# q, k and v of the neighbourhood attention projected from the transposed raw residual in fp32, with centred weights

## The reference, cut to what matters

```python
def _ln_c(v, eps=1e-06):
    m = jnp.mean(v, axis=1, keepdims=True)
    s = jnp.var(v, axis=1, keepdims=True)
    return (v - m) / jnp.sqrt(s + eps)
...
qkv = jnp.einsum('bchw,oc->bohw', x, qkv_w) + qkv_b[None, :, None, None]
qkv = qkv.reshape(B, 3, ND, d, H, W)
...
    qr = q.reshape(B, h, HEAD_DIM, L)
    ku = _unfold(kmap, dil).reshape(B, h, HEAD_DIM, KK, L)
    vu = _unfold(vmap, dil).reshape(B, h, HEAD_DIM, KK, L)
    attn = jnp.einsum('bhcl,bhcpl->bhlp', qr, ku) * SCALE
...
x = x + _L1_conv_ref(_ln_c(x), L1_conv_qkv_w, L1_conv_qkv_b, ...)
```

## Time and profile before

| | |
|---|---|
| median of 3 runs | 477.91 us (475.59 to 477.93) |
| profiled execution, its own time | 474.62 us |
| its span | 472.8 us |
| DVE busy | 403.7 us, 85% |
| PE busy | 359.8 us, 76% |
| ACT, POOL busy | 208.9 us, 136.2 us |
| mean granted clock of PE | 0.865 |

### The profile page before, as it was taken

The page is one execution under the profiler, slowest core; times in us unless marked ns, Lnnn a source line. Parts: engine busy times, 40 slices in busy tenths (PEclk is TensorE's granted clock), DMA queues, the critical chain, the costliest instruction groups (busy, mean ns, idle before and its releaser), DMA issues.

```text
span 472.8 us, 8901 instructions
## 1 busy us (share of the span) xinstructions
PE 359.8 (76%) x3276; PEld 196.9 (42%) x3276; DVE 403.7 (85%) x1349; ACT 208.9 (44%) x398; POOL 136.2 (29%) x133
## 2 busy tenths in 40 slices
PE   2856688968879656799999996680479869169996
PEld 1533543425328522356666663270134322024553
DVE  4787887898979788879999999888886888888997
ACT  1650125522310121388887883520036344128994
POOL 3630002002000000088888874021000006703442
PEclk9977879989977768899999997985589976579999
DMA  8800000000000000000000000000000000100000
GB/s 339 348 1 0 1 0 3 0 2 0 0 0 1 1 0 1 1 2 3 1 3 1 2 3 1 1 1 0 1 1 0 2 0 20 27 0 2 12 14 24
DMA packets 2859, 9.72 MB, mean 21 GB/s; under 512 B 512, under 2 KB 1152, under 8 KB 2688
## 3 DMA queue, kind: packets, MB, share of 16 engines
q1 hardware_dynamic: 1296, 5.21, 2.8%
q10 hardware_dynamic: 1008, 3.42, 1.8%
q0 software_dynamic: 512, 0.53, 0.5%
HBM read 8.63 MB, written 0.52 MB: 19 GB/s over the span
## 4 chain that ended last, share of the span: by engine, by line
PE 29%; DVE 23%; issue 4%; ACT 2%; DVEq 0%; ACTq 0%
PE bank L1366 7%; PE bank L1397 7%; PE bank L1367 7%; DVE both L880 4%; DVE hx L1265 2%; PE bank L1663 2%; DVE rs L1250 2%; PE bank L1661 2%; DVE rs L1264 2%; DVE bst L616 1%; PE bank L1423 1%; DVE xn L632 1%; DVE xn L634 1%; DVE xt L601 1%; PE bank L1330 1%
## 5 line engine op out<-in xcount | busy, mean ns | idle before, releaser
L1330 PE MATMUL bank<-xs 128*128 128x512 f16 x260 | 78.7, 468 | 51.3 <-DVE bst L616 46.4
L327 POOL TENSOR_TENSOR kvx_mem<-kvx_mem 128x512 f16<-128x512 f32 x64 | 74.3, 1163 | 100.4 <-ACT kvx_mem L459 100.4
L1330 PEld LDWEIGHTS bank<-xs 128*128 128x128 f16 x260 | 29.3, 116 | 96.3 <-DVE bst L616 47.9
L1397 PE MATMUL bank<-w_high,kvx_mem 128*128 128x64 f16 x768 | 58.0, 194 | 2.4 <-POOL kvx_mem L327 1.8
L1397 PE MATMUL bank<-w_low,kvx_mem 128*128 128x64 f16 x768 | 57.7, 193 | 0.0
L1397 PEld LDWEIGHTS bank<-w_high,kvx_mem 128*128 128x128 f16 x768 | 50.4, 98 | 13.8 <-POOL kvx_mem L327 2.2
L376 ACT ACTIVATE xt<-xn 128x256 f16<-128x256 f32 x32 | 11.7, 416 | 92.4 <-DVE xn L634 89.4
L1366 PE MATMUL bank<-xs,w_high 128*128 128x512 f16 x128 | 49.9, 390 | 3.1 <-DVE kvx_mem L934 2.6
L1397 PEld LDWEIGHTS bank<-w_low,kvx_mem 128*128 128x128 f16 x768 | 48.6, 98 | 7.0
L1367 PE MATMUL bank<-xs,w_low 128*128 128x512 f16 x128 | 49.8, 389 | 0.0
L934 DVE SCALAR_TENSOR_TENSOR kvx_mem<-kvx_mem,bank 128x512 f32<-128x512 f32 x64 | 43.6, 682 | 4.9 <-ACT kvx_mem L454 3.8
(11 more groups left out here) (346 smaller groups left out, 750.3 us busy)
## 6 DMA issues: line engine op xcount, KB each, us to landing
kvx_mem<-in_m SPq DMA_DIRECT2D x1, 2560.0 KB, 13.6
pack_l<-in_l ACTq DMA_DIRECT2D x1, 898.5 KB, 18.8
kvx_mem<-in_m SPq DMA_DIRECT2D x1, 768.0 KB, 18.6
pack_c<-in_c ACTq DMA_DIRECT2D x1, 648.0 KB, 5.7
pack_l<-in_l SPq DMA_DIRECT2D x1, 586.5 KB, 15.3
pack_x<-in_x SPq DMA_DIRECT2D x1, 512.0 KB, 5.5
pack_half<-in_half ACTq DMA_DIRECT2D x1, 512.0 KB, 7.7
pack_c<-in_c ACTq DMA_DIRECT2D x1, 512.0 KB, 14.0
```

Source lines behind the costliest of these rows:

```text
L327: nc.gpsimd.tensor_tensor(gl[:, n % DEPTH, :], gw[:, n % DEPTH, :], gh[:, n % DEPTH, :], ALU.subtract).then_inc(S["unit_low_pool"], 1)
L1330: T.matmul(bank[unused][:, :], xs[:, 0:P], xs[:, 0:512], start=True, stop=True)
L1397: mm = T.matmul(out_bank[:, at + 64 * t:at + 64 * t + 64], part[:, n % DEPTH, P * t:P * t + P], w[f"w2_{m}"][:, 64 * un:64 * un + 64], sta ...
```

## The change

- The norm of this block is no longer applied to the tiles. `early_norm` stops after step 19 in moe(0) (the factor `rstd` of tiles 0 to 7 is then known), and steps 20 to 23, `normed` and the splits of "ln2" are gone.
- The weights are centred once, early: POOL writes the matrix `center` (identity minus 1/64 in two 64x64 blocks), PE multiplies it with `qkvw` (in fp32), ACT copies the result back over `qkvw`. The fp16 high and low parts of qkvw are no longer made.
- PE transposes the raw residual in fp32, two tiles per instruction, 8 instead of 16 instructions (`residual_transposed`), the first four of them inside the last units of moe(0). ACT copies them to `x_channels` (`channels_in`).
- PE multiplies in fp32 with 64 rows per matmul, `project_raw(n)`: two matmuls (rows 0 to 63 and 64 to 127) for two tiles. The first three calls come before the last `turn_back` of moe(0).
- DVE puts factor and bias on with one operation per tile, `project_in(n)`: two operations of 192 elements for two tiles, with `rstd` as a scalar per partition. The first call stands between residual(2) and residual(3), three between the statistics of tiles 8 to 15 and their moments.
- q, k and v now lie in seven planes of `kvx_mem` (q, then k and v for each r), one per kind, so that padding is shared between neighbours. POOL sets 7 pieces of it instead of 8; ACT copies a shifted pair of k and v with one operation instead of two.

```diff
             nc.gpsimd.memset(b2s[:, :, :], 0.0).then_inc(S["consts_set"], 1)
+            nc.gpsimd.memset(center[:, :], 0.0).then_inc(S["center_set"], 1)
+            pool.wait_ge(S["center_set"], 1)
+            for h in range(2):
+                q = slice(64 * h, 64 * h + 64)
+                nc.gpsimd.memset(center[q, q], -1 / 64).then_inc(S["center_set"], 1)
+            pool.wait_ge(S["center_set"], 3)
+            pool.wait_ge(loaded["c0"], 16)
+            nc.gpsimd.tensor_tensor(center[:, :], center[:, :], K["ident"], ALU.add).then_inc(S["center_set"], 1)
             scale_weights(["wqkv"])
...
+            def channels_in(half, where):
+                act.wait_ge(S["x_T"], half + 1)
+                nc.scalar.activation(x_channels[:, 512 * half:512 * half + 512], bank[where][:, :], ACT.Copy)\
+                    .then_inc(S["x_chan"], 1)
...
+                    if m == 0:
+                        channels_in(0, 0)
                     copy_out(m, chunks - 1)
+                    if m == 0:
+                        return
...
-                for step in range(17, 24):
+                for step in range(17, 20 if m == 0 else 24):
                     early_norm(step)
                 residual(2)
+                if m == 0:
+                    dve.wait_ge(S["vec_step"], steps[0])
+                    project_in(0)
+                    residual(3)
+                    dve.wait_ge(S["acc_in"], (SPREAD.index(m) + 1) * chunks)
+                    return
...
+            def project_in(n):
+                dve.wait_ge(S["kv1_out"], n + 1)
+                for t in (2 * n, 2 * n + 1):
+                    last = V.scalar_tensor_tensor(planes(queries[:, t:t + 1, :], 3, 1, 0, C)[:, :, 0, :],
+                                                  bank[2 * (n % 3) + t % 2][:, 0:192].rearrange("p (a c) -> p a c", a=3),
+                                                  rstd[:, t:t + 1], K["qkvb"].rearrange("p (a c) -> p a c", a=3),
+                                                  ALU.mult, ALU.add)
+                last.then_inc(S["kv1_in"], 1)
...
-            ln(2, res, EPS_C)
-            for n in range(8):
-                t = slice(2 * n, 2 * n + 2)
-                dve.wait_ge(S["kv1_out"], n + 1)
-                src = bank[n % 4][:, 0:384].rearrange("p (t c) -> p t c", c=192)
-                V.scalar_tensor_tensor(q1[:, t, :], src[:, :, 0:64], 1 / WSCALE, row(K["qkvb"][:, 0:64], 2),
-                                       ALU.mult, ALU.add)
...
+            tile_stats(res, HALF, NT, signal=True)
+            for n in range(1, 4):
+                project_in(n)
+            moments(HALF, NT, EPS_C)
+            rsqrt(rstd[:, HALF:NT], veps[:, HALF:NT], HALF)
+            for n in range(4, 8):
+                project_in(n)
...
+            def project_raw(n):
+                if n % 4 == 0:
+                    pe.wait_ge(S["x_chan"], n // 4 + 1)
+                if n >= 3:
+                    pe.wait_ge(S["kv1_in"], n - 2)
+                if n == 0:
+                    pe.wait_ge(S["wc_in"], 1)
+                for h in range(2):
+                    q = slice(64 * h, 64 * h + 64)
+                    mm = T.matmul(bank[2 * (n % 3) + h][:, 0:192], x_channels[q, P * n:P * n + P], K["qkvw"][q, :],
+                                  start=True, stop=True)
+                mm.then_inc(S["kv1_out"], 1)
...
+                        if m == 0 and k == N - 2:
+                            residual_transposed(0, 0)
+                        if m == 0 and k == N:
+                            turned_second(k - 2)
+                            pe.wait_ge(S["act_out"], n0 + N)
+                            project_raw(0)
+                            turned_second(k - 1)
+                            pe.wait_ge(S["weighted"], n0 + N)
+                            project_raw(1)
+                            project_raw(2)
...
-            warm_for_norm(2, 14)
-            transposed("ln2")
+            residual_transposed(1, 6)
+            for n in range(3, 7):
+                project_raw(n)
+            keep_warm(8, unused=7)
             pe.wait_ge(S["mix_set"], 2)
...
-            keep_warm(8, unused=5)
+            project_raw(7)
             pe.wait_ge(S["kv1_in"], 8)
             pe.wait_ge(S["pbias_in"], 1)
```

More of the change, by code:

```diff
@@ L49 @@
 DIRECT = [1, 3]
-SPLIT = [("c0", "wqkv"), ("r", "rw0"), ("m0", "w1_0"), ("l1", "qkvw"), ("r", "rw1"), ("m1", "w1_1"),
+SPLIT = [("c0", "wqkv"), ("r", "rw0"), ("m0", "w1_0"), ("r", "rw1"), ("m1", "w1_1"),
          ("m1", "wu_1"), ("m1", "w2_1"), ("l2", "convw"), ("r", "rw2"), ("m2", "w1_2"), ("l2", "cbT"),
@@ L55 @@
 PACK_OF = {name: pk for pk, name in SPLIT}
-HIGHS = ["wqkv", "w1_1", "wu_1", "w2_1", "rw0", "w1_0", "qkvw", "rw1", "rw2", "w1_2", "rw3", "w1_3", "w2_3",
+HIGHS = ["wqkv", "w1_1", "wu_1", "w2_1", "rw0", "w1_0", "rw1", "rw2", "w1_2", "rw3", "w1_3", "w2_3",
          "convw", "cbT"]
@@ L270, in metaformer, with rows3, planes @@
         logit_slots = [slots[4 + n % 4] for n in range(4)] + slots[0:4] + [slots[4 + n % 4] for n in range(4)]
+        PITCH = (NT + PADX) * C
+        queries = kvx_mem[:, 0:NT * C].rearrange("p (x c) -> p x c", c=C)
+        def rows3(r, a, x):
+            at = PITCH * (1 + 2 * (1, 0, 2).index(r) + a) + C * x
+            return kvx_mem[:, at:at + NT * C].rearrange("p (x c) -> p x c", c=C)
+        def planes(first, count, tiles, c0, c1):
+            plane = first[:, 0:tiles, c0:c1]
+            (part, parts), tile, one = plane.ap
+            return bass.AP(plane.tensor, plane.offset, [[part, parts], [PITCH, count], tile, one])
         def taps(r, i, a, c0, c1):
-            first = kvx[:, r, PADX - DILS[i]:PADX - DILS[i] + NT, a, c0:c1]
+            first = rows3(r, a, -DILS[i])[:, :, c0:c1]
             (part, parts), (tile, tiles), (one, cols) = first.ap
@@ L495, in _ @@
                                      accum_out=small[:, 8 + j:9 + j]).then_inc(S["gexp_ready"], 1)
+            act.wait_ge(S["centred"], 1)
+            nc.scalar.activation(K["qkvw"], bank[4][:, 0:192], ACT.Copy).then_inc(S["wc_in"], 1)
             split("ln1")
@@ L501, in _ @@
             moe(0)
+            channels_in(1, 6)
             load_table(ACT.Exp)
-            split("ln2")
             for n, (i, r) in enumerate(SHIFTS):
                 act.wait_ge(S["shift_out"], n + 1)
-                for kv in range(2):
-                    nc.scalar.activation(kvx[:, r, PADX:PADX + NT, kv, 16 * i:16 * i + 16],
-                                         bank[4 + n % 4][:, :].rearrange("p (x a c) -> p x a c", a=2, c=16)[:, :, kv, :],
-                                         ACT.Copy).then_inc(S["shift_in"], 1)
+                nc.scalar.activation(planes(rows3(r, 0, 0), 2, NT, 16 * i, 16 * i + 16),
+                                     bank[4 + n % 4][:, :].rearrange("p (a x c) -> p a x c", a=2, c=16),
+                                     ACT.Copy).then_inc(S["shift_in"], 1)
             for r in range(3):
@@ L1341, in split_weights, with residual_transposed @@
                     pe.wait_ge(S["weight_low_vec"], VEC_LOWS.index(name) + 1)
+            def residual_transposed(half, where):
+                for i in range(4):
+                    if half == 0 and i == 0:
+                        pe.wait_ge(S["acc_in"], 2)
+                        pe.wait_ge(S["act_out"], first_unit[0] + 13)
+                    if half == 1 and i % 2 == 0:
+                        pe.wait_ge(S["acc_in"], 3 + i // 2)
+                    t = 8 * half + 2 * i
+                    mm = T.transpose(bank[where][:, P * i:P * i + P], res[:, t:t + 2, :], ident)
+                mm.then_inc(S["x_T"], 1)
+            def project_raw(n):
[10 more added lines that the diff above has]
+                mm.then_inc(S["kv1_out"], 1)
             def moe(m):
@@ L1545, in _ @@
                 mm.then_inc(S["wf_out"], 1)
+            pe.wait_ge(S["center_set"], 4)
+            pe.wait_ge(loaded["l1"], 16)
+            T.matmul(bank[4][:, 0:192], center, K["qkvw"], start=True, stop=True).then_inc(S["centred"], 1)
             warm_for_norm(1, 20)
```

47 lines of the change are left out of this document (21 added, 26 removed).

## The result

The changed kernel takes 469.84 us (median of four executions, 469.36 to 470.51), the kernel before 477.37 (four, 475.59 to 477.93): 7.5 us less, a ratio of 0.985 with a 95% interval of 0.982 to 0.988. The prediction had 474.0 and a range of 471.0 to 476.6. The two profiled executions are 5.05 apart: 474.62 before, 469.57 now, spans 472.8 and 467.8, mean granted clock .865 and .864.

What follows compares the result with a forecast made beforehand. VectorE's list was taken to bound the stage: 6.55 us off, 1.1 dearer operations and 1.7 waiting give 3.75, taken as 3.8 off the median 477.91, so 474.0 us; range 471.0 to 476.6.

Steps and rivals of the forecast that it cites:

- The list of DVE: VectorE up to the first product of q and k: 6.55 us removed, sixteen changed operations 1.1 us dearer.
- the scalar's surcharge: VectorE's operation putting q, k, v on: a scalar per partition adds 0.07 us, giving 0.335 for each.
- The new wait: VectorE ahead of residual(3), for the last turn_back behind project_raw calls priced at 0.7 us each: 1.7 us of waiting.
- the four transposes: TensorE between the last turn_back but one and the biases: four more transposes cost 0.56 us.
- rival 2: Row halves of project_raw overlap: 0.35 us per call, residual(3) 1.05 earlier, 4.8 us gained; chance 20%.
- The base: Forecast time: the gain of 3.8 us counted off the median of the runs, 477.91, not the profiled execution's 474.62.
- Rival 3: project_raw(7) comes late, 1.4 us, behind eight unread matmuls at half clock; gain 2.4 us; chance 15%.
- Rival 4: Sixteen operations cost the dear end, or several tile-shape changes cost twice; gain 1 to 2 us; chance 9%.
- Rival 5: Half clock over the shifts and ten unread matmuls makes the sums late: 3.4 us slower, 481.3; chance 6%.
- the other edits at nothing: Centring product, dropped low part of qkvw, padding and the single shifted copy on ACT: costed at nothing.
- The distance of the sums: TensorE's sums of the logits start no later than 11.6 us after the first product, still waiting for DVE.

Runs made afterwards that it cites:

- Experiment 2: Changed kernel, but with subtraction and scaling back on DVE, transposing normed tiles, factor constant 1, all project_raw calls behind the last turn_back: 471.30 us, ratio 0.990 to the kernel before.
- experiment 1: Changed kernel with one fp32 matmul of 128 rows and 384 columns on block-diagonal weights instead of two of 64 rows and 192 columns: 473.46 us, ratio 0.994.
- experiments 3 and 4: Kernel before with 5 instead of 14 unread matmuls (475.00 us) and unchanged (475.12); then changed kernel repeated beside kernel before: 470.41 against 476.03, 469.54 against 474.81.
- experiment 7: Changed kernel with project_raw(1) and (2) behind the last turn_back and project_in of tiles 2 to 7 dealt between short statistics steps: 471.34 us, ratio 0.989.
- experiment 6: Changed kernel without its eight unread matmuls ahead of the product for the bias: 471.26 us, ratio 0.989 to the kernel before.
- experiment 5: Changed kernel with project_raw(1) and (2) put behind the last turn_back: 470.23 us, ratio 0.988; on a second chip 470.05 against the changed kernel's 469.54.

## Why the prediction was off

**The list of DVE** held. (The stage of the kernel before has three holes of DVE with a releaser, 0.22, 0.49 and 0.63, not two; all three lie in the part taken off, so the sum is not touched.) The 6.55 us taken off, the 16 operations at 0.335 (0.34 measured) and the short steps left in place leave 10.32 us without a wait (12.02 less 1.7); the measured 10.77 less its wait of 0.46 is 10.31. Experiment 2 confirms the scalar's surcharge.

**The new wait was mis-sized: this step failed.** The prediction has "a call (two matmuls, four instructions) 0.65; the weight load, which a 192-column matmul does not cover fully, makes me take 0.7". A call issues in 0.33. For three calls ahead of the last turn_back that is 1.1 us of the 1.24 by which the wait is shorter. The remaining 0.1 is the four transposes, priced too high: from the last turn_back but one to the biases it is 0.75 (96.16 to 96.91) and not 0.31 + 0.56. So the stage gives 5.1 instead of 3.8. Engine, place and releaser of the wait were right. The prediction had set the overlap of the column halves aside since no row showed it for row halves, and given it 20% as rival 2 (4.8 us, wait 0.6); experiment 1 shows it. The Trainium skill, TensorEngine Tiling (Array Packing), Key Properties, says that tiles of a split array work independently and in parallel. The trace agrees: 0.33 against 0.64 to 0.70 in full shape, with 0.006 to 0.007 us between the starts of the two halves. Its other half, that a change of tiling mode drains the engine, fits 0.19 a change, as expected.

**The base was the second step that failed, and the one that put the time below the range**: "The same 3.8 off the median gives **474.0 us**." With the right gain and this base it would have been 472.8, inside the range. The median of three was taken as the place from which the gain counts, though the profiled execution lay 3.3 below it. Off the profile's own time the same gain gave 470.8, and with 5.1 it gives 469.5, where 469.84 was measured. The kernel has a spread of 4 us of its own (experiments 3 and 4), and the first median stood high in it: 477.91, where the medians of the later calls are 474.8 to 476.0. That the profiled execution lay close to these was luck, known only from those calls; one execution is no better a base by right than three. The range took that spread in only below rival 2, and only part of it (473.1 less the 2.3 of the runs would be 470.8, not 471.0).

**Rival 3** did not happen here; its mechanism showed itself in experiment 7, where the stage has 0.9 us less of VectorE's work and waits ahead of that point. **Rival 4** (dear operations) did not happen. **Rival 5**'s condition did not come about; experiment 6 brought a smaller form of it and the slack of 2.07 took it, as worked out. Strides, POOL's work and the other edits at nothing cost nothing that the stage shows, and at the last early step the changed kernel's profile is not behind. The distance of the sums, 11.56, stayed the 11.6 that was given.

Open: why an execution has its clock fall at one place and not another, and with it how much of a microsecond gained in this stage reaches the end. No version tried is faster than the changed kernel by more than the spread.

## What to carry to other kernels

When the profiled execution lies far from the median of a few, the kernel has a spread: take more executions before choosing the base, count from both times, and let the range hold both. Where a neighbouring row shows two halves of the array at work together, price a split in the other direction by both values and let the range hold them. Freed time on one engine changes when the others are idle: in experiment 7's profile VectorE's list is 0.6 us shorter than in experiment 5's, and TensorE's clock falls over the next eight matmuls, which it does not do there. One profile of each doesn't prove that the one causes the other. And compare stages before totals: the totals of two profiles here differ by up to 2.9 us at one place 270 us behind the change.

## What the runs showed of the hardware

- An fp32 product of 64 rows by 192 columns in two row halves issues in 0.33 us for both halves, and in 0.64 (0.70 with the start of a group) as one full-shape product of 384 columns; the matmuls of the two halves start 0.006 to 0.007 apart. The row halves overlap fully.
- A scalar per partition costs VectorE 0.07 us on 192 elements from PSUM (0.27 and 0.34 from start to start).
- Short dependent steps of VectorE (128x8) follow each other after 0.20 us; with an independent operation of 192 elements between them that operation starts 0.08 after the first step, and step and operation together take 0.40 instead of 0.54 (experiment 7).
- The 32 products of one row (1x256, fp16) in the codebook stage take 13.4 to 16.3 us from first to last start, by the pair at which TensorE's clock falls: 0.64 a pair at the full clock, 1.07 at the half.
- The same program has a spread of 4 us in 475, and a long and a short execution differ in the granted clock at short products (.67 and .78 from 170 to 180 us), not in the stage looked at.
